# Channel search of a fused attention block: layer norm's squares taken as tile products on the matrix engine, and 59 second counts on the activation engine, each placed between the second and third first count

## The reference, cut to what matters

```python
x = x + xattn(layernorm(x), ctx_4096)     # x: 16 x 64 x 2048, ctx_4096: 16 x 1601 x 2048
x = x + attn(layernorm(x), wq, wk, wv, wo)
x = x + ffn(layernorm(x), ...)

# in xattn, for every batch and each of the 2048 positions:
_, topk_idx = top_k(cm, 38)               # 38 largest of 1601 context values
mask = zeros(..., 64); mask[topk_idx] = 1 # an index of 64 or more falls outside and sets nothing
crucial, rest = mask * x, (1 - mask) * x  # then max and mean of each, a small convolution, a gate

def _layernorm(x, axis=-1, eps=1e-05):
    m = mean(x); v = var(x)
    return (x - m) / sqrt(v + eps)
```

## Time and profile before

| | |
|---|---|
| median of three runs | 2226.02 us |
| profiled execution, its own time | 2228.47 us |
| its span in the profile | 2226.5 us |
| busy over the span: PE, DVE, ACT, POOL | 1926.3, 1314.7, 1124.3, 1025.6 us |
| the search, in which the change lies | to 657 us |

### The profile page before, as it was taken

How to read it: one execution, slowest core, us unless ns; L and a number is a source line. 1 busy time by engine, 2 the same in 40 slices (tenths; PEclk the granted TensorE clock), 3 DMA queues, 4 the chain that set the end, 5 groups by cost and what they waited for, 6 DMA issues and landing times. The chain is left out here.

```text
span 2226.5 us, 37959 instructions
## 1 busy us (share of the span) xinstructions
PE 1926.3 (87%) x14353; PEld 1554.5 (70%) x14353; DVE 1314.7 (59%) x2065; ACT 1124.3 (50%) x2527; POOL 1025.6 (46%) x911
## 2 busy tenths in 40 slices
PE   4677788777752648999999999999999999999999
PEld 4666666655640246788878888888878878788887
DVE  5999999999899988644435601244455326631111
ACT  7999998998956665433233422232323323422222
POOL 2222233332227505666555546556645445544554
PEclk9999999999885869999999999999999999999999
DMA  9999998999922025522235443222254355334443
GB/s 387 398 383 389 346 330 321 329 330 323 340 91 91 19 75 173 156 81 80 85 128 180 134 139 107 89 78 80 88 189 143 114 168 178 131 118 137 146 137 112
DMA packets 158390, 407.58 MB, mean 183 GB/s; under 512 B 15616, under 2 KB 44544, under 8 KB 156544
## 3 DMA queue, kind: packets, MB, share of 16 engines
q1 hardware_dynamic: 157920, 403.52, 51.6%
q0 software_dynamic: 288, 1.64, 0.2%
HBM read 379.93 MB, written 25.17 MB: 182 GB/s over the span
## 5 line engine op out<-in xcount | busy, mean ns | idle before, releaser
L1408 POOL TENSOR_TENSOR t<-t,t 128x512 fp32r<-128x512 f32 (+1 forms) x488 | 653.3, 1351 | 670.2 <-ACT t L1401 599.7
L1957 PE MATMUL ps<-t,t 128*128 128x512 f32 x1856 | 734.4, 396 | 14.8 <-POOL t L1408 9.4
L1959 PE MATMUL ps<-t,t 128*128 128x512 f32 x1856 | 723.4, 390 | 0.0
L1958 PE MATMUL ps<-t,t 128*128 128x512 f32 x1856 | 722.8, 389 | 0.0
L1401 ACT ACTIVATE t<-t 128x512 fp32r<-128x512 f32 (+1 forms) x488 | 293.7, 609 | 697.0 <-PE ps L1959 373.8
L786 PE MATMUL ps<-t,t 128*128 128x128 bf16 (+1 forms) x6097 | 420.4, 226 | 178.0 <-DVE t L471 169.3
L786 PEld LDWEIGHTS ps<-t,t 128*128 128x128 bf16 x6097 | 370.3, 102 | 265.7 <-DVE t L471 223.7
L471 DVE TENSOR_SCALAR t<-t,t 128x1601 bf16<-128x1601 f32 x469 | 480.5, 1054 | 14.2 <-PE ps L786 9.7
L699 ACT ACTIVATE t<-t,t 128x1601 bf16<-128x1601 f32 x256 | 417.0, 1629 | 33.5 <-DVE t L636 29.7
L1957 PEld LDWEIGHTS ps<-t,t 128*128 128x128 f32 x1856 | 348.4, 188 | 94.2 <-POOL t L1408 14.0
L1959 PEld LDWEIGHTS ps<-t,t 128*128 128x128 f32 x1856 | 348.4, 188 | 73.7
(11 more groups left out here) (240 smaller groups left out, 1796.7 us busy)
## 6 DMA issues: line engine op xcount, KB each, us to landing
t<-ctxT SPq DMA_DIRECT2D x256, 800.5 KB, 7.0
t<-wqkv SPq DMA_DIRECT2D x192, 256.0 KB, 3.1
t<-wo SPq DMA_DIRECT2D x128, 256.0 KB, 4.6
t<-wb SPq DMA_DIRECT2D x128, 256.0 KB, 3.6
t<-xT SPq DMA_DIRECT2D x48, 256.0 KB, 7.1
t<-x1d SPq DMA_DIRECT2D x32, 256.0 KB, 4.9
x2d<-t SPq DMA_DIRECT2D x32, 256.0 KB, 2.0
t<-x2d SPq DMA_DIRECT2D x8, 1024.0 KB, 7.2
```

The lines of the kernel that those rows point to most:

```text
L1408: e.tensor_tensor(wlo[r][:, 0:nk, :], raw[r][:, 0:nk, :], wh[r][:, 0:nk, :].bitcast(F32), ALU.subtract).then_inc(w_lo, 1)
L1957: e.matmul(bank[:, :], wh[r][:, q, :], xl, start=(kt == 0), stop=False)
L1958: e.matmul(bank[:, :], wlo[r][:, q, :], xh, start=False, stop=False)
L1959: m = e.matmul(bank[:, :], wh[r][:, q, :], xh, start=False, stop=(c == NCH[p] - 1 and q == nk - 1))
```

## The change

Four edits, all in the search:

1. `by_act` holds for every group from 1 to 59. Sixteen second counts go from VectorE masks (and their TensorE products) to ScalarE.
2. On ScalarE the second count moves from behind the fourth first count to between the second and the third, and the read-out of slot 3 of the step before moves from behind the first first count to behind the second, in all steps with such a count. GpSimd's decision moves with it to the end of its own step.
3. The squares are no longer made by ScalarE. TensorE multiplies each centred 128 x 128 piece of a tile by itself (four products for a tile, one after another in the step's four places), so that the wanted sums stand on the diagonal; VectorE multiplies the total by the identity and sums each row (128 x 512, then 4 values). `LN0_SUB`'s subtractions go to the steps in which no batch is ended.
4. Steps of `fin_vector` move behind third-count masks of their step, `maxima` waits for an earlier part of the batch end, and SyncE's load of row numbers no longer waits for the squares.

```diff
 def by_act(g):
-    return 1 <= g < NQ - 4 and not (25 <= g + 1 <= 56 and g % 2 == 0)
+    return 1 <= g < NQ - 4
...
             if n == RID_TILE:
-                e.wait_ge(ln0_sqsum, 2 * NT)
+                e.wait_ge(set_up, 3)
...
-    LN0_SUM, LN0_MEAN, LN0_SUB, LN0_VAR = (15, 30), (23, 39), (24, 40), (43, 58)
+    LN0_SUM, LN0_MEAN, LN0_SUB, LN0_VAR = (15, 31), (23, 39), (24, 40), (42, 58)
...
     def ln0_vector(e, i):
-            x, j = XN[:, h, :, :], (i - LN0_SUB[h]) // 2
-            if LN0_SUB[h] <= i < LN0_SUB[h] + 16 and (i - LN0_SUB[h]) % 2 == 0:
+            x, d = XN[:, h, :, :], i - LN0_SUB[h]
+            if 0 <= d < 16 and d % 4 < 2:
+                j = 2 * (d // 4) + d % 4
...
-            if i == LN0_VAR[h] + 1:
-                e.wait_ge(ln0_turned, 2 * h + 1)
-                e.tensor_scalar(ln0_inv[h], ln0_sums[h][:, 0:4], 1.0 / L, EPS, ALU.mult, ALU.add).then_inc(ln0_var, 1)
+            if i == LN0_VAR[h]:
+                products = ln0_rs[h][:, :].rearrange("p (c n) -> p c n", n=128)
+                e.wait_ge(ln0_sqsum, h + 1)
+                e.wait_ge(ln0_sub, 8 * h + 8)
+                e.tensor_tensor(products, ln0_sums[h][:, :].rearrange("p (c n) -> p c n", n=128),
+                                ident.rearrange("p (a n) -> p a n", a=1).to_broadcast([128, 4, 128]), ALU.mult).then_inc(ln0_var, 1)
+                e.wait_ge(ln0_var, 4 * h + 1)
+                e.tensor_reduce(ln0_inv[h], products, AX.X, ALU.add).then_inc(ln0_var, 1)
+                e.wait_ge(ln0_var, 4 * h + 2)
+                e.tensor_scalar(ln0_inv[h], ln0_inv[h], 1.0 / L, EPS, ALU.mult, ALU.add).then_inc(ln0_var, 1)
...
     def ln0_scalar(e, i):
-            t = i - LN0_SUB[h] - 1
-            if 0 <= t < NT:
...
-                e.activation(lsq[:, :], XN[:, h, t, :], ACT.Square).then_inc(ln0_sq, 1)
...
     def ln0_tensor(e, i, u):
-            t = i - LN0_SUB[h] - 2
-            if 0 <= t < NT and u == 0:
-                e.wait_ge(ln0_mean, h + 1)
-                e.wait_ge(ln0_sq, 16 * h + t + 1)
-                e.matmul(ln0_sums[h][:, :], ones, lsq[:, :], start=(t == 0), stop=(t == NT - 1)).then_inc(ln0_sqsum, 1)
...
+            t = i - LN0_SUB[h] - 1
+            if 0 <= t < NT:
+                if u == 0:
+                    e.wait_ge(ln0_mean, h + 1)
+                    e.wait_ge(ln0_sub, 8 * h + t // 2 + 1)
+                x = XN[:, h, t, 128 * u:128 * u + 128]
+                m = e.matmul(ln0_sums[h][:, 128 * u:128 * u + 128], x, x, start=(t == 0 and u == 0), stop=(t == NT - 1 and u == 3))
...
     def sign_scalar(e, i, u):
-        if u == 0 and by_act(i - 2):
-            e.wait_ge(b_signed, ACT_NO[i - 2] + 1)
+        if u == 2 and by_act(i - 1):
+            e.wait_ge(b_signed, ACT_NO[i - 1] + 1)
...
     def search_scalar(e):
-                if u == 0 and 2 <= i:
+                if u == by_act(i - 2) and 2 <= i:
                     counts_scalar(e, i - 1, 3)
-                if 1 <= i <= NQ + 1:
-                    for v in {2: [0], 3: [1]}.get(u, []):
-                        counts_scalar(e, i, v)
-            if by_act(i - 1):
-                sign_b_scalar(e, i - 1)
+                if u == 1 and by_act(i - 1):
+                    sign_b_scalar(e, i - 1)
+                if 2 <= u and 1 <= i <= NQ + 1:
+                    counts_scalar(e, i, u - 2)
             ln0_scalar(e, i)
             if 1 <= i <= NQ + 1:
                 counts_scalar(e, i, 2)
```

More of the change, by code:

```diff
@@ L570, in ln0_scalar @@
                 e.activation(Mn[:, :], ln0_sums[h][:, :], ACT.Copy, scale=1.0 / L).then_inc(ln0_mean, 1)
-            t = i - LN0_SUB[h] - 1
-            if 0 <= t < NT:
[L573 to L577, removed]
-                e.activation(lsq[:, :], XN[:, h, t, :], ACT.Square).then_inc(ln0_sq, 1)
[L579 to L583, removed]
             if i == LN0_VAR[h] + 1:
-                e.wait_ge(ln0_var, 2 * h + 1)
+                e.wait_ge(ln0_var, 4 * h + 3)
                 e.activation(ln0_inv[h], ln0_inv[h], ACT.Sqrt).then_inc(ln0_std, 1)
             if i == LN0_VAR[h] + 2:
-                e.wait_ge(ln0_var, 2 * h + 2)
+                e.wait_ge(ln0_var, 4 * h + 4)
                 for c in range(4):
@@ L591, in ln0_scalar @@
             if i == LN0_VAR[h] + 3:
-                e.wait_ge(ln0_turned, 2 * h + 2)
+                e.wait_ge(ln0_turned, h + 1)
                 e.activation(ln0_rs[h][:, :], ln0_sums[h][:, :], ACT.Copy).then_inc(ln0_rstd, 1)
@@ L602, in ln0_tensor @@
                     m.then_inc(ln0_total, 1)
-            t = i - LN0_SUB[h] - 2
-            if 0 <= t < NT and u == 0:
-                e.wait_ge(ln0_mean, h + 1)
-                e.wait_ge(ln0_sq, 16 * h + t + 1)
-                e.matmul(ln0_sums[h][:, :], ones, lsq[:, :], start=(t == 0), stop=(t == NT - 1)).then_inc(ln0_sqsum, 1)
[L608 to L612, removed]
+            t = i - LN0_SUB[h] - 1
[5 more added lines that the diff above has]
+                m = e.matmul(ln0_sums[h][:, 128 * u:128 * u + 128], x, x, start=(t == 0 and u == 0), stop=(t == NT - 1 and u == 3))
+                if t == NT - 1 and u == 3:
+                    m.then_inc(ln0_sqsum, 1)
             if i == LN0_VAR[h] + 3 and u == 0:
-                e.wait_ge(ln0_flat, 5 * h + 5)
+                e.wait_ge(ln0_flat, 4 * h + 4)
                 e.matmul(ln0_sums[h][:, :], ones, ln0_rs[h][:, :], start=True, stop=True).then_inc(ln0_turned, 1)
@@ L631, in maxima @@
                 if half == 0 and b >= 2 and t0 == 0:
-                    e.wait_ge(fin, NF * (b - 1))
+                    e.wait_ge(fin, NF * (b - 2) + 7)
+                    e.wait_ge(tied, 4 * (b - 1))
                     e.wait_ge(kept, 2 * (b - 1))
@@ L666, in search_vector @@
                     e.wait_ge(b3_dec, ACT_NO[c] + 1)
-                end_batch([] if first_steps else [7])
                 w = insB[:, 4 * c:4 * c + 4]
                 e.copy_predicated(vc[:, :, 0], w, vc[:, :, 2]).then_inc(b_set, 1)
-                end_batch([] if first_steps else [8, 9])
                 e.wait_ge(b_set, c + 1)
@@ L687, in search_vector @@
                     end_batch([2 + k - first])
+                if not first_steps and k in (3, 4, 5):
+                    end_batch([k + 4])
                 if k == 4:
@@ L705, in sign_b_scalar @@
         e.wait_ge(a_set, g + 1)
-        e.wait_ge(signed, 4 * g + 8)
+        e.wait_ge(signed, 4 * g + 6)
         e.activation(scr[:, :], ring[n % NR][:, :], ACT.Sign, bias=v8[:, b % 2, t, 1:2], scale=-SHRINK,
@@ L768, in search_gpsimd @@
         for i in range(NQ):
-            if by_act(i - 2):
-                decide_b_gpsimd(e, i - 2)
             copy_gpsimd(e, 4 * i)
@@ L775, in search_gpsimd @@
             copy_gpsimd(e, 4 * i + 2)
+            if by_act(i - 1):
+                decide_b_gpsimd(e, i - 1)
         e.tensor_copy(nT[:, NT * (B - 1):], v8[:, (B - 1) % 2, :, 3]).then_inc(kept, 1)
@@ L820, in ln0_out @@
         e.wait_ge(ln0_rstd, h + 1)
-        e.wait_ge(ln0_sq, 16 * h + 16)
         e.tensor_tensor(x, x, bc(ln0_rs[h][:, :], tiles), ALU.mult).then_inc(signal, 1)
```

## The result

The changed kernel takes 2239.96 us (median of 4, 2238.35 to 2240.70) against 2225.90 (2225.61 to 2226.99): a ratio of 1.0059 as recorded (the two medians alone give 1.0063), 95% interval 1.0043 to 1.0075. It is slower, as forecast, but by 14.1 us where 6.5 were forecast, and it lies just above the range (2239). The profiled execution took 2240.70 us, its span is 2238.6.

The account below looks back on a forecast made before the run. ScalarE was taken to bound steps 3 to 23 and 56 to 60, VectorE 24 to 55; +0.4 + 8.2 - 3.4 + 2.8 - 1.5 = +6.5 us took the median from 2226.0 to 2232.5, range 2220 to 2239.

Parts of the forecast that it names:

- ScalarE's step is 0.39 us longer by its neighbours: Search steps on ScalarE: the new order makes more direct neighbours wait for accumulators, 9.67 us a step instead of 9.28.
- Rival 1: ScalarE's step stays at 9.28 us; steps 24 to 55 gain 11.0, sum -13.3, 2212.7 us; chance 0.13.
- ScalarE takes over the bound in steps 24 to 55: Steps 24 to 55: ScalarE's 38.7 us for four steps exceeds VectorE's 37.1, so ScalarE sets 309.4 us.
- (a): Batch end on VectorE, steps 24 to 55: 1.6 us stop every fourth step, priced at 0.07 us a step, 2.2 in all.
- (b): The variance on VectorE at step 42, ahead of a mask ScalarE wants: +1.8 us; the same at step 58.
- (c): TensorE's four quarter products for squares take 1.6 us a step; waits in steps 31 to 38 cost 2 us in all.
- Rival 3: TensorE's quarters at 3.8 us a step make read-outs late and cancel the gain in steps 24 to 55; 2237 to 2243; chance 0.15.
- The moved batch-end parts at nothing: VectorE's batch-end parts moved later in the step; with earlier `maxima` and row-number load 0, between -1 and +1 us together.
- Behind step 61, -1.5: Behind steps 56 to 60, the read-out ahead of step 61 no longer stands behind a second count of 1.61 us: -1.5 us.
- Behind the search, nothing: Everything behind the search is the same code with the same data, so no change of its own there.
- rival 2: Gain and loss meet: ScalarE waits for nobody, -3.1 us, or +1.7 with half the waits; 2223 to 2230.4; chance 0.27.
- Five steps at 9.67: Steps 56 to 60 on ScalarE without waits, counted as +0.7 us in the sum of rival 2.

Follow-up runs that it names:

- e3: The changed kernel with the read-out of slot 3 back behind the first first count, the second count staying between second and third: 2224.91 us.
- e4: The changed kernel with VectorE's batch-end steps two masks later in their step, ScalarE's order left as changed: 2226.52 us.
- e1: The changed kernel with ScalarE's and GpSimd's order as before the change, all 59 second counts and TensorE's squares kept: 2202.40 us.
- e5: e1 with only the 43 second counts of the kernel before on ScalarE, so without the sixteen added ones: 2217.42 us.
- e7: The changed kernel with 20 small identity products on TensorE ahead of the mask sums behind VectorE's stop, in 7 of 14 batch ends: 2234.80 us.
- e9: The kernel before with only the moved batch-end parts on VectorE and the earlier condition of `maxima`: 2218.30 us.
- e11: e1 with the batch end on VectorE back where it was before the change: 2209.75 us.

## Why the prediction was right and wrong

The mechanism that the forecast rests on was right, and so was the direction. One wait was priced far too low, and in one stretch it was left out. That is more than the whole miss (12.1 us in the spans where 6.5 were forecast), since other terms were too high.

- *ScalarE's step is 0.39 us longer by its neighbours*: right. 9.70 us after, in steps without a wait, in steps 3 to 23 and in 24 to 55; e3 and e4, in which nothing else of the order's cost is left, stand at 9.66 to 9.70 over steps 3 to 23, e1 and e5 at 9.27 to 9.28. Rival 1 fell with it, and so did the alternative by the overlap of 93 ns, which the Trainium skill ("ScalarE: Activation LUTs", What ACT_TABLE_LOAD costs) gives without a condition: the traces agree with it where the next instruction doesn't wait for the accumulator, and only there. Rival 1's gain was what e1 has, by the old order.
- *ScalarE takes over the bound in steps 24 to 55*: right. It is busy for 304.81 of 322.57 us (94.5%, where over 95% was forecast); VectorE fell from 309.29 to 295.23, 91.5%, as forecast.
- *(a) The stop at the batch end costs 0.07 us a step, 2.2 us in steps 24 to 55*: **the step that failed.** In steps 3 to 23 the forecast didn't have the stop at all; it has only the small waits of before there, 0.07 us a step or 1.5 us. The stop was found and rightly sized (1.6 us; 21.0 us in 13 stops), and its place in VectorE's queue too. Its price was taken as VectorE's lateness alone. Without the stop (e3) the five batch ends of steps 3 to 23 give 5.3 us (208.93 to 203.67) and the eight of steps 24 to 55 give 8.6 (322.57 to 313.94), so 1.1 us each; with the stop and the clock held up (e7) the first five give 4.6 (to 204.30). The missing mechanism is that the mask sums behind the stop can run at TensorE's lower clock, shown by e7. The granted clock of the earlier trace rows, 0.95, 0.96 and 0.89, said that TensorE was at its lower level for a part of the search already, and the forecast had no term for it.
- *(b) The variance at steps 42 and 58, +1.8 each*: about right in size. The product took 0.68 us and the sum 0.69, and both steps took 11.99 us where other such steps took 10.48: +1.5.
- *(c) Quarters of products, 1.6 us a step, and 2 us lost in steps 31 to 38*: too high. Four quarters take about 1.2 us, and steps 31 to 38 are no longer than their neighbours. Rival 3 (quarters from 3 us a step) fell. Its sign, waits of ScalarE over 10 us in steps 24 to 55, was nearly there (9.1 us for TensorE) for another reason. Of what the prediction takes from the Trainium skill ("TensorE: Matmul & The Clock Gate"), the price by columns stands in LDWEIGHTS, and that 32-bit weights have no faster way in the section behind it, Weight-path perf modes. No row here prices a load by itself; a quarter's two loads and two products fitted into 0.31 us.
- *The moved batch-end parts at nothing, -1 to +1*: wrong against the kernel before, by 7 to 8 us (e9; e1 against e11). It isn't what made the forecast too low, since the forecast of steps 24 to 55 was built up from ScalarE's instructions, without a gap at the batch mask. The changed kernel with the old batch end was not run; by these two runs its steps 24 to 55 would have been longer still.
- *Behind step 61, -1.5*: -3.3 in the windows, and what else shortened them was not tried. *Behind the search, nothing*: +0.2.

With (a) at its measured price the forecast would have been 6.7 + 5.3 = +12.0 in steps 3 to 23 (measured +12.6) and, with (c) at nothing, 313.0 + 1.8 + 8.6 = 323.4, +1.0, in steps 24 to 55 (measured +0.2). The range's upper end had been set by rival 3, which was the wrong mechanism at about the right size. That the measured time lies so near to the range is luck in that sense.

Some slips of the prediction changed nothing in its sum. The accumulator's read ends 0.09 us behind the end of its count, not 0.19 (134.12 + 0.20 against 132.60 + 1.63). Five steps at 9.67 are +0.6 and not +0.7. The parts of rival 3 add up to +18.9 and not +17, and rival 2's +1.7 would be 2227.7, so its upper end of 2230.4 is only where the forecast's own case begins.

## What to carry to other kernels

Where an engine's accumulated results are waited for by its own next instruction, the order of its queue has a price: put something between two such instructions, and count the direct neighbours before a move. When a change adds an idle stretch to an engine that feeds TensorE, price not only the stretch but what TensorE does behind it; here a stop of 1.6 us cost ScalarE a wait of 0.3 to 0.6 us where the clock stayed up, and of 0.7 to 2.4 us where the products behind it ran at half the clock. And undo the parts of a change one at a time before giving it up: this one held a part worth 1.1% under an order that cost more.

## What the runs showed of the hardware

- In step 14 of the changed kernel TensorE's granted clock was 1.00 to 146.50, at the end of an idle stretch of 1.99 us, 0.50 from 147.00 on, still 0.51 from 149 to 157, with another idle stretch of 1.48 us that ended at 150.86, and 1.00 from 158. With that second stretch filled by 20 small products (e7) it was 0.90 from 148 to 156. Thirteen 128 x 128 bf16 products took 1.4 to 1.5 us at the lower level, against 0.87.
- An ACTIVATE with an accumulator that waits for the one before it starts 0.2 us later than one that doesn't: 1.80 to 1.82 against 1.61 us behind a count of 1601 values, 0.44 against 0.25 behind a read-out of 128. No run changed the wait alone, but likeness of the neighbours doesn't do it: behind the search the changed kernel has ACTIVATEs of one kind with an accumulator in a row, each of which waits for the one eight places before it, and they start 0.24 us apart:

```profile
670.70 0.21 ACT L801 ACTIVATE ps<-t 128x64 f32<-128x64 f32 x1
...
670.94 0.20 ACT L801 ACTIVATE ps<-t 128x64 f32<-128x64 f32 x1
```

- A 128 x 128 product in f32 on its own tile, with both weight loads, takes about 0.3 us of TensorE at the higher clock (from 327.13 to the next product's start at 327.44), so 1.2 us for a tile's four, where one 128 x 512 product took 0.94:

```profile
327.13 0.47 PE L603 MATMUL ps<-t 128*128 128x128 f32 x2
327.44 1.02 PE L594 MATMUL ps<-t,t 128*128 128x512 f32 x2
```
